# Six-layer attention and FFN stacks: the norms' spreads ahead of the transpositions, and the norms' split as a plain difference on GpSimd

## The reference, cut to what matters

```python
def l2norm(t):
    return t / jnp.maximum(jnp.linalg.norm(t, axis=-1, keepdims=True), 1e-12)
def attn_layer(x, Wqkv, qs, ksc, Wo):            # 16 heads of 64
    q, k, v = heads(x @ Wqkv)
    q = l2norm(q) * qs
    k = l2norm(k) * ksc
    q = q * cos * scale + rotate_half(q) * sin * scale
    k = k * cos / scale + rotate_half(k) * sin / scale
    out = local_attention(q, k, v)               # windows of 32: own and previous
    return out @ Wo
def ffn_layer(x, g, bln, W1, b1, W2, b2):
    xn = layernorm(x) * g + bln
    a, gate = jnp.split(xn @ W1 + b1, 2, -1)
    return a * gelu(gate) @ W2 + b2
for i in range(6):
    x = attn_layer(shift_tokens(x), ...) + x
    x = ffn_layer(shift_tokens(x), ...) + x
```

## Time and profile before

| | |
|---|---|
| median of 3 runs | 4420.13 us (4412.47 to 4425.89) |
| profiled execution | 4411.89 us |
| its span | 4410.1 us |
| TensorE busy | 4119.1 us (93%) |
| VectorE busy | 3484.4 us (79%) |
| ScalarE busy | 3076.0 us (70%) |
| GpSimd busy | 1802.7 us (41%) |

### The profile page before, as it was taken

How to read it: one execution, slowest core, us unless ns; L and a number is a source line. 1 busy time by engine, 2 the same in 40 slices (tenths; PEclk the granted TensorE clock), 3 DMA queues, 4 the chain that set the end, 5 groups by cost and what they waited for, 6 DMA issues and landing times. The chain is left out here.

```text
span 4410.1 us, 111762 instructions
## 1 busy us (share of the span) xinstructions
PE 4119.1 (93%) x43089; PEld 2408.1 (55%) x43089; DVE 3484.4 (79%) x4981; ACT 3076.0 (70%) x7032; POOL 1802.7 (41%) x1071
## 2 busy tenths in 40 slices
PE   7997999999999999999967589999999999999998
PEld 3443555555555555555536445555555555555554
DVE  5775888888888888888735478888888888888886
ACT  3555777777777777777762267777777777777776
POOL 3112444444444444444404534444444444444442
PEclk7999999999999999999986699999999999999999
DMA  2213444444443444444300044434434444444342
GB/s 43 30 21 80 100 107 97 102 103 94 106 107 84 109 103 99 101 103 99 74 10 3 3 119 102 106 90 110 105 87 108 101 104 94 100 102 106 90 97 54
DMA packets 232516, 380.72 MB, mean 86 GB/s; under 512 B 59364, under 2 KB 122336, under 8 KB 231688
## 3 DMA queue, kind: packets, MB, share of 16 engines
q1 hardware_dynamic: 231560, 372.20, 36.3%
q10 hardware_dynamic: 384, 0.79, 0.1%
HBM read 39.22 MB, written 1.05 MB: 9 GB/s over the span
## 5 line engine op out<-in xcount | busy, mean ns | idle before, releaser
L835 POOL TENSOR_TENSOR b_prob<-b_prob,b_rinv 128x768 f32<-128x768 f32 x384 | 564.9, 1471 | 1857.9 <-DVE b_rinv L1262 1857.9
L841 POOL TENSOR_TENSOR b_prc<-b_prc,b_sws 128x1024 f32<-128x1024 f32 x384 | 910.8, 2372 | 64.3 <-DMA b_sws<-b_prs 64.1
L1130 ACT ACTIVATE b_prob<-ps,b_nmx 128x96 f32<-128x96 f32 x3072 | 751.2, 363 | 0.0
L879 PEld LDWEIGHTS ps<-ident,b_prob 128*128 128x128 f32 x3072 | 377.5, 141 | 421.7 <-issue 302.4
L1203 DVE SCALAR_TENSOR_TENSOR b_prc<-ps,b_qks,b_rot 128x512 f32<-128x512 f32 x768 | 571.2, 744 | 10.6 <-ACT b_sq L1091 10.2
L1205 DVE SCALAR_TENSOR_TENSOR b_prs<-ps,b_qks,b_rot 128x512 f32<-128x512 f32 x768 | 570.3, 743 | 0.0
L1243 DVE TENSOR_TENSOR b_prc<-b_prc,ps 128x512 f32<-128x512 f32 x384 | 264.2, 688 | 381.7 <-PE ps L937 307.4
L1216 DVE SCALAR_TENSOR_TENSOR b_rsp<-b_rhi,b_minus_hi,b_rn 128x512 fp32r<-128x512 f32 x192 | 412.3, 2147 | 110.6 <-ACT b_rn L1077 110.6
L879 PE MATMUL ps<-ident,b_prob 128*128 128x128 f32 x3072 | 464.8, 274 | 5.3 <-ACT b_pT L1066 5.3
L1111 ACT ACTIVATE b_oT<-ps 128x512 f32<-128x512 f32 x384 | 227.0, 591 | 341.9 <-PE ps L895 341.9
L1066 ACT ACTIVATE b_pT<-ps 128x512 f32<-128x512 f32 x724 | 435.6, 602 | 15.1 <-PE ps L879 10.9
(11 more groups left out here) (292 smaller groups left out, 7295.7 us busy)
## 6 DMA issues: line engine op xcount, KB each, us to landing
b_sws<-b_prs SPq DMA_DIRECT2D x1536, 128.0 KB, 2.3
b_vs<-b_va SPq DMA_DIRECT2D x384, 256.0 KB, 3.8
b_wqkv<-in_L_ffn_Wqkv SPq DMA_DIRECT2D x96, 192.0 KB, 3.6
b_xs<-y SPq DMA_DIRECT2D x126, 128.0 KB, 2.5
b_wo<-in_L_ffn_Wo SPq DMA_DIRECT2D x96, 64.0 KB, 3.1
b_xs<-y SPq DMA_DIRECT2D x42, 127.8 KB, 2.3
b_rot<-in_rot SPq DMA_DIRECT2D x2, 2048.0 KB, 7.8
b_w<-in_L_ffn_W SPq DMA_DIRECT2D x24, 170.5 KB
```

The lines of the kernel that those rows point to most:

```text
L835: pool.tensor_tensor(prob[:, r, :, P - KEYS:P], prob[:, r, :, P - KEYS:P], rinv[:, r % 2, :].rearrange("p (b a) -> p b a", a=1).broadcast_ ...
L841: pool.tensor_tensor(prc[:, r, :, :], prc[:, r, :, :], sws[:, r % 2, :, :], ALU.add)\
L879: t = pe.transpose(bank[6][:, i * P:(i + 1) * P], prob[:, kd, 4 * e + 2 * h + m, :], ident[:, :])
L1130: g = act.activation(prob[:, kb, i, P - KEYS:P], wide[0][:, e * CH + m * KEYS:e * CH + (m + 1) * KEYS], ACT.Exp, bias=nmx[:, kb % 2, i:i + 1])
```

## The change

Three things.

1. In all slots but the Gelu slots TensorE does the two spreads before the first transposition, and the first mask between the k matmul and the second transposition. In Gelu slots the order stays.
2. `rhi` is made with a bias by row (`low_back`): on the rows that are to keep the rounded value it is -1000, so that the exponential is 0 there. The split is then the plain difference `rn - rhi`, and the operand `minus_hi` goes.
3. The split moves to GpSimd, into the odd slot in which the norms are made, between its two operations; only behind Gelu slots it stays on VectorE, in the even slot after, as a plain difference too. Of the 192 splits 148 move and 44 stay.

```diff
--- before
+++ after
@@ gpsimd slot @@
-                    v, u = unit(1), unit(3)
+                    w_, v, u = unit(0), unit(1), unit(3)
                     if u:
 ...
+                    if w_ and j % 2 and ffn(unit(FLAG + 1))[0] != 5:
+                        pool.wait_ge(S["rn_done"], ONE + twos(w_) + 1)
+                        pool.tensor_tensor(rsp[:, :], rn[:, :], rhi[:, :].bitcast(F32), ALU.subtract).then_inc(S["split_done"], 1)
                     if v:
 ...
@@ tensor @@
+                def mask(kb, e, pe=pe):
+                    pe.matmul(wide[0][:, e * CH:e * CH + 4 * KEYS], identb[:, :], band[:, 1 if kb % 2 else 0, :],
+                              start=True, stop=False, skip_group_check=True)
 ...
                     if d:
                         UD, kd = um(d)
+                    if d and before == 5:
                         turn(UD, kd, 0)
 ...
                             .then_inc(S["nb_mm"], 1)
+                    if d and before != 5:
+                        turn(UD, kd, 0)
                     key_bank_free(f0)
                     if a:
                         pe.wait_ge(S["pk_done"], ONE + U)
                         pe.matmul(bank[1][:, :], W[:, 1, :], X, start=True, stop=True).then_inc(S["k_mm"], 1)
-                    if d:
+                    if d and before == 5:
                         turn(UD, kd, 1)
                     if b:
                         pe.wait_ge(S["exp_done"], ONE + UB)
-                        for e in range(2):
-                            if e:
-                                pe.wait_ge(S["kn_done"], ONE + UB + 1)
-                            pe.matmul(wide[0][:, e * CH:e * CH + 4 * KEYS], identb[:, :], band[:, 1 if kb % 2 else 0, :],
-                                      start=True, stop=False, skip_group_check=True)
+                        mask(kb, 0)
+                    if d and before != 5:
+                        turn(UD, kd, 1)
+                    if b:
+                        pe.wait_ge(S["kn_done"], ONE + UB + 1)
+                        mask(kb, 1)
@@ scalar @@
-                        act.activation(rhi[:, :], rn[:, :], ACT.Exp, bias=ss_back[:, 0:1], scale=-0.5).then_inc(S["hi_done"], 1)
+                        act.activation(rhi[:, :], rn[:, :], ACT.Exp, bias=low_back[:, 0:1], scale=-0.5).then_inc(S["hi_done"], 1)
@@ vector @@
-                    if b and j % 2 == 0:
+                    if b and j % 2 == 0 and ffn(unit(FLAG + 2))[0] == 5:
                         n = twos(b)
                         dve.wait_ge(S["rn_done"], ONE + n + 1)
-                        dve.scalar_tensor_tensor(out=rsp[:, :], in0=rhi[:, :].bitcast(F32), scalar=minus_hi[:, 0:1], in1=rn[:, :],
-                                                 op0=ALU.mult, op1=ALU.add).then_inc(S["split_done"], 1)
+                        dve.tensor_tensor(rsp[:, :], rn[:, :], rhi[:, :].bitcast(F32), ALU.subtract).then_inc(S["split_done"], 1)
@@ constants @@
-    t["minus_hi"] = np.where(np.arange(P)[:, None] % 4 < 2, 0.0, -1.0).astype(np.float32)
+    t["low_back"] = np.where(np.arange(P)[:, None] % 4 < 2, -1000.0, SS_BACK).astype(np.float32)
```

4 lines of the change are left out of this document (2 added, 2 removed).

## The result

| | before | after |
|---|---|---|
| median of 5 runs each | 4422.49 us (4412.47 to 4431.07) | 4390.53 us (4375.31 to 4393.15) |
| ratio | | 0.9919, 95% interval 0.9901 to 0.9938 |
| profiled execution, its span | 4411.89, 4410.1 us | 4391.85, 4390.1 us |
| TensorE busy | 4119.1 us (93%) | 4085.5 us (93%) |
| VectorE busy | 3484.4 us (79%) | 3200.4 us (73%) |

A forecast was written before the change was run, and what follows sets the result against it. TensorE was taken to set the pace. Ten full layers at 5.0 us, 3.6 in first layers' last slots and 8.8 from pairs without FFN made 62 us: 4350 profiled, 4358 as median, range 4320 to 4396.

The forecast's parts named there:

- Part 1, the plain slot: New TensorE order in plain slots: the second mask no longer waits for VectorE's key product, gaining 0.16 us a slot.
- The 4 Gelu slots: Gelu slots keep the old order but gain 0.16 us each, as L1243 gets GpSimd's sum earlier from the slot before.
- Slots 4 and 20 at 0.44: FFN variance matmul waits for VectorE, whose chain starts 0.44 us earlier and passes that on; 0.9 us a layer.
- Slots 5, 10, 26 at nothing: No gain: behind Gelu slots (10, 26) VectorE is still busy; with FFN step 2 strips wait as the mask did.
- Slot 16: Behind an FFN end y_add comes late, with the spreads now first: a loss of 0.3 us.
- Part 2: The held split leaves VectorE: slots 2 and 18 gain 0.6 us each, 1.2 us a layer; remaining 44 splits gain nothing.
- Part 3: Split on GpSimd, about 1.2 us, hidden in FFN slots; pairs without FFN fall from 16.99 to 16.44 us, gaining 0.55.
- Behind the wait for `rn_done` nothing new is late: GpSimd's new wait for the norms costs nothing, since L835 ends after they are made in most odd slots.
- The signs: Right: mask wait below 40 us, L1243 0.44 us earlier, 44 VectorE splits. Wrong: copy-released gaps, pairs above 17 us, longer y_add waits.
- The second transposition waits for the copy: Rival: second transposition waits for ScalarE's copy until 3.03, not 2.78, costing 0.25 us in 340 slots; 4443 us, chance 0.08.
- GpSimd binds more widely: Rival: the split costs 2.35 us, so pairs without FFN and slots 2 and 18 lose; 4394 us, chance 0.14.
- Nothing comes through: Rival: TensorE waits again later in the slot and the held split was never last; 4420 us, chance 0.10.

The follow-up runs named there:

- e2_order: Against the kernel before, only the new order on TensorE, the split staying on VectorE in its old form: 4396.12 us, ratio 0.9957.
- e8_late: The changed kernel with the old TensorE order in slots 16 and 0 of a layer: 4383.3 us, ratio 0.9914 to before.
- e3_gpsimd: The changed kernel with TensorE back in the old order, so only the split's part of the change: 4413.01 us, ratio 0.9989 to before.
- e5_start: The changed kernel with the splits of each stack's first slots left on VectorE: 4373.69 us, ratio 0.9901 to before.
- e6_double: The changed kernel with GpSimd's split done twice, 1.27 us more in each of 148 odd slots: 4454.71 us, ratio 1.0077 to before.

## Why the prediction was right, and where not

- **Part 1, the plain slot, right.** The planned starts came within 0.01 us, and the 0.16 us of every plain and odd slot came through. e2_order shows that it is the order that gives it.
- **"The 4 Gelu slots" at 0.16, mis-sized:** 0.04 to 0.05 in slots 9, 15 and 25, 3 us too much in the ten layers (and slots 31 and 0 gained nothing, below). I had argued that L1243 gets GpSimd's sum earlier there; what ends these slots I had not read, and it stays open.
- **Slots 4 and 20 at 0.44, right in size and half right in cause.** Slot 4 gets it from the order alone (8.46 in e2_order), slot 20 only with both parts (8.94 and 8.89 alone, 8.46 together).
- **Slots 5, 10, 26 at nothing, right. Slot 16, right in size:** +0.33 for +0.3. The cause is wider than I wrote: the first spread waits 0.95 us for the held split and only then the second 0.42 us for y_add. And e8_late shows that undoing it gains nothing.
- **Part 2, "0.6 us for each" of slots 2 and 18, right:** 0.64 and 0.55 in the medians (0.44 each in the mean), and L1253 is released there by GpSimd's sum, as said. The split alone gives 0.53 (e3_gpsimd). The mean is smaller because 7 of these 20 slots were already quick before: in them the split started ahead of GpSimd's sum or clear of it, took its 740 ns, and the slot took 7.58 to 7.75 us. In the other 13 it started behind the sum and was held, and the slot took 8.19 to 8.68. So the profile before already had both cases side by side, 0.6 us apart. One of the quick ones, timeline of before:

```profile
1144.00 0.74 DVE L1216 SCALAR_TENSOR_TENSOR b_rsp<-b_rhi,b_minus_hi,b_rn 128x512 fp32r<-128x512 f32 x1
...
1144.22 2.75 POOL L841 TENSOR_TENSOR b_prc<-b_prc,b_sws 128x1024 f32<-128x1024 f32 x1 [0.74 <-DMA b_sws<-b_prs]
```

It is the slot of the earlier trace rows: that row already showed a slot without the hold, in which GpSimd's sum comes last. The 0.6 itself was picked between 0 and 1.61 us without a working, so that it fits so well is in part luck.
- **Part 3, right.** The split takes 1.27 us for the estimated 1.2, and the pair 16.46 for 16.44. But the 8.8 us counted 16 pairs. Slots 6 to 18 hold 13 of them, 7.2 us by this price, and gave 5 to 7; slots 2 to 5 gave none, even where the start's wait is gone (+0.3 in e5_start). In the changed kernel's first layers, slots 5, 9, 13 and 17 take up to 0.9 us longer than the other odd ones. There a sum waits for its swap DMA (0.70 us at 479.23 in slot 9, and L1253 then 1.91 us for the sum). "SyncE's swap DMAs wait for the sum and shift with it" was put at nothing in the sum and was not nothing.
- **The step that failed:** "Behind the wait for `rn_done` nothing new is late: L835 ends after the norms are made in most odd slots." In the first slots of a stack there is no L835. The rotary sum, queued behind the new wait, came late: 7.1, 7.8 and 8.7 us in slots 2 to 5 of the three profiles, back at 0.3 in e5_start. The rule that a new wait holds what is queued behind it was applied to the steady slots alone.
- **The account:** 8.8 (start) - 5.8 (pairs) - 2.4 (rest of the first layers) - 44.3 (28 slots of ten layers) = -44 us, where I had -62. Of the some 18 us, 9 are the start (7 the wait and 2 the clock in slot 1), 3 the pairs, 1 the first layers, 5 the gains that I had counted in slots 0, 19 and 31, where DMAs or the loop's turn end last; within the 28 slots the misses nearly cancel (Gelu slots and slots 2 and 18 gave 7 us less, slots 1, 4, 5, 10, 17, 20 and their like 6 more). The loop turns took another 4 to 10 us, which I had not foreseen (below). With them the three profiles are by these columns 34, 38 and 29 us shorter in the stacks than before's, beside 36, 37 and 42 us by the three ratios: a rough match, as the ratios rest on many executions and each profile on one. The sum was too high by these terms; the range was wide enough for 36 us as well as for 62.
- **VectorE's busy time, down by about 350 us in the forecast:** the split's line went from 412.3 us to 81.9, 330 less, and the engine's busy time fell by 284. The profile lets neighbouring operations overlap a little, and with 148 fewer of them there is less overlap, so the sum falls more than the busy time.
- **The signs.** One was missed: the second mask's wait was to fall below 40 us and is 66 for the load, 89 with the matmul. The first slots of the stacks, slots 2 and 18 and the Gelu slots keep theirs. The others came: L1253 0.43 us earlier in the plain slot (1.60 for 2.03), 44 splits on VectorE, 148 of 1.27 us on GpSimd, more than 73 us of waiting for the sum. Of the signs against it none did; TensorE waits 26 us more for y_add at the second spread's load, less than it gained.
- **The rivals.** "The second transposition waits for the copy" did not come: 0.22 us of room, [0.33] on the load and no gap in the matmuls. Its price leaves out a term that it needs: 2.55 + 0.43 is 2.98, and the 3.03 takes in the 0.05 us between the copy's end (1504.37) and the load (1504.42) in the earlier trace rows. "GpSimd binds more widely" was in its price too low: with a split of 2.5 us (e6_double) the kernel is 70 us slower than changed, so at 2.35 it would have ended on the slower side (estimate: 1.08 / 1.27 of 70, 60 us above), not at 4394. I had left out slots 4 and 20. "Nothing comes through" holds nearly for one half of the change, the split alone (ratio 0.9989), and not for the other.
- **GpSimd against VectorE.** GpSimd's 1272 ns are 1.9 times VectorE's undisturbed 681, about the factor that the Trainium skill gives (GPSIMD Engine Reference, Performance versus the Vector engine). The median on VectorE is 2353, held by GpSimd, so here the slower engine is the quicker place. The changed kernel's own lines:

```profile
L840 POOL TENSOR_TENSOR b_rsp<-b_rn,b_rhi x148: 1262/1272/1282, 419.0 to 4305.0; 128x512 fp32r<-128x512 f32 x148
...
L1227 DVE TENSOR_TENSOR b_rsp<-b_rn,b_rhi x44: 1845/1860/1919, 628.9 to 4325.9; 128x512 fp32r<-128x512 f32 x44
```

## What to carry to other kernels

When an engine gets a new wait, go through the first and last slots of each stage as well as the steady one: there the work that covers the wait is missing. Two edits may each stand in the way of the other's gain; here 23 and 9 us apart were 44 together, so a part that gives little alone is not yet worth nothing. Before moving work to an idle engine, ask whose next operation waits for that engine's round: GpSimd was busy only 45% of the time, and yet 1.27 us more on it in 148 slots cost 70 us in all, because its round ended last, or nearly, in four slots of 32 and in those without FFN work.
